# A Mamba block with an FP4 feed-forward on eight cores: other queues for the stores, and two buffers in the output projection

## The reference

```python
xn = _layernorm(x, axis=-1)
x = x + attn(xn) + ffn(xn)

# attn ("Mamba"): D_MODEL 1024, D_INNER 2048, D_STATE 16, DT_RANK 64, D_CONV 4
x = _rmsnorm(resid, norm_w)
skip = x @ skip_w.T
x = silu(_causal_depthwise_conv(x @ in_w.T, conv_w, conv_b))
delta = softplus(x @ wd1.T @ wd2.T + wd2_b)
Bm, Cm = x @ wb.T, x @ wc.T
y = _selective_scan(x, delta, Bm, Cm, A)      # h = exp(dt*A)*h + dt*x*B ; y = h.C
y = (y + x * W_D) * silu(skip)
return resid + y @ out_w.T

# ffn: every operand is quantized to FP4 in blocks of 16 and back
h = silu(fp4_linear(x, w_gate)) * fp4_linear(x, w_up)
return fp4_linear(h, w_down)
```

## Time and profile before

| | |
|---|---|
| median of 3 runs | 10604.0 us (10601.94 to 10607.22) |
| the profiled execution | 10596.79 us, of it the span of the slowest core 10595.3 us |
| spans of the 8 cores | 10570.5 to 10595.3 us |
| busy share of the span | DVE 58%, PE 27%, ACT 21%, POOL 10% |
| chain that ended last | DVE 56%, PE 13%, DMA 11%, issue 9%, ACT 9% |

### The profile page before, as it was taken

One profiled execution on the slowest core, in us unless ns is written; L12 is line 12 of the kernel. 1 busy time (PEld: TensorE's weight loads), 2 busy tenths in 40 slices (PEclk: granted clock), 3 DMA queues, 4 the chain that ended last, 5 costly groups with the idle time before them and its releaser, 6 DMA issues.

```text
span 10595.3 us, 50685 instructions; the slowest of 8 cores (10570.5 to 10595.3 us)
## 1 busy us (share of the span) xinstructions
PE 2895.6 (27%) x8880; PEld 961.4 (9%) x8880; DVE 6135.6 (58%) x5976; ACT 2235.5 (21%) x2910; POOL 1017.9 (10%) x680
## 2 busy tenths in 40 slices
PE   1111125545430333311111113333322222222224
PEld 0000011111110000000000001111000000000001
DVE  5656653434431222279999982222189997999940
ACT  1222211111123111123333321111122222222200
POOL 0000000000000000034444430000000000000000
PEclk9999996766665555555555556666555555555557
DMA  1111210010011100010000001111111112112122
GB/s 49 45 46 44 61 57 12 12 47 34 30 33 42 42 33 34 32 57 24 16 24 16 16 28 71 42 43 42 70 52 46 38 48 81 54 54 71 54 66 73
DMA packets 194274, 460.18 MB, mean 43 GB/s; under 512 B 114416, under 2 KB 115056, under 8 KB 170736
## 3 DMA queue, kind: packets, MB, share of 16 engines
q1 hardware_dynamic: 155760, 312.99, 9.3%
q0 software_dynamic: 38208, 143.94, 3.7%
HBM read 296.71 MB, written 160.17 MB: 43 GB/s over the span
## 4 chain that ended last, share of the span: by engine, by line
DVE 56%; PE 13%; DMA 11%; issue 9%; ACT 9%; DVEq 1%; ACTq 1%; SPq 0%; POOLq 0%
DVE s3o_hb L54 11%; DVE pf_ub L54 8%; DVE pf_E L54 6%; DVE s3o_ub L54 5%; DVE s3o_hcb L54 3%; PE c3o_pssk L825 2%; PE c3p_psx L759 2%; DVE c3o_cb L54 2%; DVE c3p_cb L54 2%; DVE q_t L54 2%; DMA sdelta<-c3p_db 2%; DMA sdelta<-c3o_db 2%; DVE p2q_t L54 1%; PE c_pso L1266 1%; PE c3o_psx L759 1%
## 5 line engine op out<-in xcount | busy, mean ns | idle before, releaser
L54 DVE TENSOR_TENSOR_SCAN s3o_hb<-s3o_ab,h_sb,s3o_ub 128x2048 bf16<-128x2048 f32 x256 | 1147.8, 4484 | 83.3 <-ACT s3o_ab L103 57.9
L54 POOL TENSOR_TENSOR pf_ub<-pf_dxt,pf_Brep 128x1536 f32<-128x1536 f32 x256 | 792.0, 3094 | 1022.1 <-DVE pf_E L54 761.0
L54 DVE TENSOR_TENSOR pf_ub<-pf_dxt,pf_Brep 128x512 f32<-128x512 f32 x256 | 802.6, 3135 | 26.7
L103 ACT ACTIVATE s3o_ab<-s3o_dt,A_sb 128x2048 f32<-128x2048 f32 x256 | 513.2, 2005 | 1426.4 <-DVE s3o_hb L54 1397.1
L103 ACT ACTIVATE pf_E<-pf_c,pf_bias,nA_sb 128x2048 f32<-128x2048 f32 x256 | 536.8, 2097 | 980.4 <-DVE pf_E L54 962.5
L1015 PE MATMUL s3o_psht<-eye_sb 128*128 128x128 bf16 x768 | 203.3, 265 | 1868.5 <-DVE s3o_hb L54 1163.6
L1198 PE MATMUL pf_psht<-eye_sb 128*128 128x128 bf16 x768 | 201.5, 265 | 1602.6 <-DVE pf_ub L54 1054.6
L54 DVE TENSOR_TENSOR s3o_ub<-s3o_dxt,s3o_Brep 128x2048 f32<-128x2048 f32 x256 | 586.8, 2292 | 27.0 <-DVE s3o_hcb L54 0.5
L54 DVE SCALAR_TENSOR_TENSOR pf_E<-pf_E,pf_ub 128x2048 f32<-128x2048 f32 x256 | 586.9, 2293 | 26.8
L103 ACT ACT_TABLE_LOAD x180 | 230.9, 1283 | 1477.2 <-PE p_psu L584 311.7
L54 DVE TENSOR_TENSOR p_h<-p_h,p_psu 128x512 f32<-128x512 f32 (+1 forms) x96 | 61.8, 644 | 746.1 <-ACT p_h L103 746.1
(11 more groups left out here) (175 smaller groups left out, 6156.5 us busy)
## 6 DMA issues: line engine op xcount, KB each, us to landing
s3o_dt<-sdelta SPq DMA_DIRECT2D x32, 1024.0 KB, 6.5
s3o_xct<-sxc SPq DMA_DIRECT2D x32, 1024.0 KB, 5.4
sxc<-c3p_xc POOLq DMA_DIRECT2D x64, 256.0 KB, 2.6
sdelta<-c3p_db POOLq DMA_DIRECT2D x64, 256.0 KB, 2.6
pf_dt<-sdelta SPq DMA_DIRECT2D x16, 1024.0 KB, 4.8
pf_xct<-sxc SPq DMA_DIRECT2D x16, 1024.0 KB, 4.8
sxc<-c3o_xc POOLq DMA_DIRECT2D x64, 256.0 KB, 2.6
sskip<-c3o_skb POOLq DMA_DIRECT2D x64, 256.0 KB, 2.6
```

What stands on the lines that cost most here:

```text
L54: instr = attr(*a, **k)
L103: scalar.activation(out=out, in_=in_, func=func, **kw).then_inc(kb.sems["S"], 1)
```

## The change

1. **Stores of the quantized weights** (stage 1) are started by ACT, right behind its last copy into `wide`, and counted on `Stg`; before, SP started them and counted on `St`. SP's load of `xb` still waits for `St`, which no longer counts them.
2. **Stores of `sxc`, `sskip`, `sB`, `sC`, `sdelta`, `sypart`, `sym`** (stages 4, 6, 7) are started by SP and counted on `St`; before, by POOL on `Stg`. The waits follow, and the one ahead of the copy into `dlowb` is gone.
3. **Output projection**: `outwT` is loaded by POOL into two buffers in turn; `ymt`, `rtile`, `ob` and the PSUM tiles exist twice. The load of tile `tt` waits for PE and DVE of tile `tt-2`, and for no store.

```diff
@@ gen_p0b
-            @B.sync
-            def _(sync):
-                kb.wait(sync, "S", ev)
-                kb.dma(sync, dst.rearrange(...)[...], wide[:].rearrange(...)[...], sem="St")
-            st_done = kb.cnt["St"]
+            @B.scalar
+            def _(scalar):
+                kb.wait(scalar, "S", ev)
+                kb.dma(scalar, dst.rearrange(...)[...], wide[:].rearrange(...)[...], sem="Stg")
+            st_done = kb.cnt["Stg"]
@@ feed-forward, before the loads of wgh, wuh, wdh
                 kb.wait(sync, "St")
+                kb.wait(sync, "Stg")
@@ p3_chunks, behind the first loop
                 sba.wait("Tn", t_dl)
-                sba.wait("Stg")
                 sba.act(dlowb[:], ps_dl[:], AF.Copy)
@@ p3_chunks, delta loop (sxc, sskip, sB, sC, sypart and sym likewise)
                     sba.wait("V", v_zb2)
-                    sba.wait("Stg")
+                    sba.wait("St")
                     sba.act(db[:], zb[:], AF.Exp)
                     s_db = sba.act(db[:], db[:], AF.Ln, bias=1.0)
 
-                    @B.gpsimd
-                    def _(gpsimd):
-                        kb.wait(gpsimd, "S", s_db)
-                        kb.dma(gpsimd, sdelta[...], db[:], sem="Stg")
+                    @B.sync
+                    def _(sync):
+                        kb.wait(sync, "S", s_db)
+                        kb.dma(sync, sdelta[...], db[:], sem="St")
@@ output projection, loads of outwT
-            @B.sync
-            def _(sync):
-                kb.wait(sync, "V")
-                kb.wait(sync, "S")
-                kb.wait(sync, "St")
-                kb.wait(sync, "Tn")
-                kb.dma(sync, tmpc[:], outwT.rearrange(...)[:, et, :])
+            @B.gpsimd
+            def _(gpsimd):
+                kb.wait(gpsimd, "V", oc_done[j])
+                kb.dma(gpsimd, oww_tmp[j][:], outwT.rearrange(...)[:, et, :], sem="Lg")
@@ output projection, token tiles
             @B.sync
             def _(sync):
-                kb.wait(sync, "V")
-                kb.wait(sync, "St")
-                kb.wait(sync, "Stg")
-                kb.dma(sync, ymt[:], sym.rearrange(...)[...])
-                kb.dma(sync, rtile[:], racc[tt * 128:(tt + 1) * 128, :])
+                kb.wait(sync, "Tn", t_os[j])
+                kb.wait(sync, "V", v_os[j])
+                if tt < 2:
+                    kb.wait(sync, "St")
+                kb.dma(sync, ymt[j][:], sym.rearrange(...)[...])
+                kb.dma(sync, rtile[j][:], racc[tt * 128:(tt + 1) * 128, :])
```

More of the change, by code:

```diff
@@ L807, in p3_chunks @@
                     v_xcf = kb.cnt["V"]
-                    @B.gpsimd
-                    def _(gpsimd):
-                        kb.wait(gpsimd, "S", s_xc)
-                        kb.dma(gpsimd, sxc[et * 128:(et + 1) * 128, c0:c0 + CH], xcb[:], sem="Stg")
+                    @B.sync
+                    def _(sync):
+                        kb.wait(sync, "S", s_xc)
+                        kb.dma(sync, sxc[et * 128:(et + 1) * 128, c0:c0 + CH], xcb[:], sem="St")
                     @B.tensor
@@ L832, in p3_chunks, with _ @@
                         sba.wait("Tn", t_bc)
-                        sba.wait("Stg")
+                        sba.wait("St")
                         s_sk = sba.act(skb[:], ps_sk[:], AF.Silu)
[L836 to L839, removed]
+                        @B.sync
+                        def _(sync):
+                            kb.wait(sync, "S", s_sk)
+                            kb.dma(sync, sskip[et * 128:(et + 1) * 128, c0:c0 + CH], skb[:], sem="St")
                 t_dl = kb.cnt["Tn"]
@@ L849, in p3_chunks, with _ @@
                 s_dl = sba.act(bcb[:, CH:2 * CH], ps_C[:], AF.Copy)
[L851 to L855, removed]
+                @B.sync
+                def _(sync):
+                    kb.wait(sync, "S", s_dl)
+                    kb.dma(sync, sB[:, c0:c0 + CH], bcb[:, 0:CH], sem="St")
+                    kb.dma(sync, sC[:, c0:c0 + CH], bcb[:, CH:2 * CH], sem="St")
                 for et in range(ET):
@@ L1036, in p3_scan, with _ @@
                             sba.flush(B)
[L1038 to L1041, removed]
+                            @B.sync
+                            def _(sync):
+                                kb.wait(sync, "S", s_y)
+                                kb.dma(sync, sypart[et * 128:(et + 1) * 128, :], ytl[:], sem="St")
                         else:
@@ L1059, in p3_scan, with _ @@
                             v_ym = kb.cnt["V"]
[L1061 to L1064, removed]
+                            @B.sync
+                            def _(sync):
+                                kb.wait(sync, "V", v_ym)
+                                kb.dma(sync, sym[et * 128:(et + 1) * 128, :], ymb[:], sem="St")
                     sba.flush(B)
@@ L1226, in build_nc @@
         oww = sb("c4_oww", [128, ET, D], BF16)
[L1227 to L1231, removed]
-        for et in range(ET):
-            @B.sync
-            def _(sync):
-                kb.wait(sync, "V")
-                kb.wait(sync, "S")
-                kb.wait(sync, "St")
-                kb.wait(sync, "Tn")
-                kb.dma(sync, tmpc[:], outwT.rearrange("(a p) d -> p a d", p=128)[:, et, :])
-            ldv = kb.cnt["L"]
+        oww_tmp = [sb(f"c4_owt{j}", [128, D]) for j in range(2)]
+        oc_done = [kb.cnt["V"], kb.cnt["V"]]
+        for et in range(ET):
+            j = et % 2
+            @B.gpsimd
+            def _(gpsimd):
+                kb.wait(gpsimd, "V", oc_done[j])
+                kb.dma(gpsimd, oww_tmp[j][:], outwT.rearrange("(a p) d -> p a d", p=128)[:, et, :], sem="Lg")
+            ldv = kb.cnt["Lg"]
             @B.vector
@@ L1261, in _ @@
                 kb.wait(tensor, "L", ldy)
-                kb.wait(tensor, "V")
-                kb.wait(tensor, "S")
+                kb.wait(tensor, "V", v_os[j] if v_os[j] else v_oww)
                 for ds in range(2):
                     for et in range(ET):
-                        mi = tensor.matmul(ps_o[ds][:], ymt[:, et, :],
+                        mi = tensor.matmul(ps_o[j][ds][:], ymt[j][:, et, :],
                                            oww[:, et, ds * 512:(ds + 1) * 512],
```

59 lines of the change are left out of this document (34 added, 25 removed).

## The result

The changed kernel takes 10403.2 us (median of 8 runs) against 10603.9 in the same comparison: a ratio of 0.981, 95% interval 0.980 to 0.982. That is 201 us off, where the prediction said 215 (10389, range 10325 to 10462). The profiled execution has a span of 10402.8 us on its slowest core, core 1; before it was core 5.

| stage, core 5 | before, us | after, us | difference | forecast |
|---|---|---|---|---|
| weights and first norm | 1465.5 | 1415.5 | -50.0 | -37 |
| feed-forward | 1632.2 | 1631.1 | -1.1 | 0 |
| norm of the prefix | 316.5 | 315.0 | -1.5 | 0 |
| projection of the prefix | 1092.8 | 1030.3 | -62.5 | -74.5 |
| state of the prefix | 1818.3 | 1819.8 | +1.5 | 0 |

A forecast was written before the change was run, and what follows sets the result against it. No engine is full; in the projections ACT waits for `sdelta` stores to land. Terms 122 + 27 + 37 + 8 + 18 + 3 = 215 us off 10596.8 give 10381.8, with the median 7.2 above: 10389, range 10325 to 10462.

The forecast's parts named there:

- What bounds the delta loop: Both projections: the next Exp waits for the `sdelta` store to land; the store alone closes a 4.72 us pass.
- The start: Delta loop: SP starts the store 0.12 us after Ln, POOL 0.59, so a pass gains 0.47 us.
- The landing: Delta loop: `sdelta` lands from SP in 2.05 us, not 2.6; with the sooner start, 122 us over 120 passes.
- the sign to look for: Delta loop: a pass of about 3.7 us in place of 4.72, with SP starting 0.12 us behind Ln.
- Rival 1: Delta loop: landing on SP stays at 2.6 us, so the loop gives 56 us; 146 in all, 10458; chance 0.17.
- The ends of the first loops: Both projections: shorter waits for the last store, sooner `sB` and `sC`; 27 us, ends 16 and 32.
- Stage 1: Token tile's load no longer waits for the weight store's landing: 37 us, at most 49, at worst 0.
- The 0.6 us for two transfers side by side: Stage 1: a 256 KB store moving at the same time may hold the token tile's load 0.6 us.
- Rival 2: Stage 1 and output projection's token tiles: side-by-side transfers hold each other up fully; 160 us in all, 10444; chance 0.10.
- The output projection: 8 us gained ahead of the first matmul, and 18 us between token tiles, 1.2 a tile, 15 times.
- The covers: Scan and state of the prefix: 0, wrong beyond 5 us; ACT loses 0 by issuing 52 stores more.
- The waits at the ends of stages: Three ends of stages, where SP waits for the last store, give 1 us each: 3.

The follow-up runs named there:

- e6: The changed kernel with two buffers for `db`, so that Exp waits for the store before the last: 10220.1 us, ratio 0.965.
- e10: The changed kernel with ACT starting the `sdelta` stores itself, its instructions emitted pass by pass, not one block for 16 passes: 10551.2 us in one run.
- e5: The changed kernel with each `sdelta` store split into two of 128 KB, one after the other: 10578 us in one run.
- e7: The changed kernel with the output projection's loads of tile `tt+1` ahead of tile `tt`'s store in SP's queue: 10246.9 us, ratio 0.967.
- e4: The changed kernel with SP again starting the quantized-weight stores, on the counter that the token tile's load does not wait for: 10409.9 us.

## Why the prediction was right, point by point

- **What bounds the delta loop** was right, and e6 shows it directly: with the wait for the landing moved away by one store, a pass falls from 4.03 to 2.48 us, which Exp, Ln and `zb` close.
- **The start** was right: 0.13 us for SP and, in e10, for ACT, against the 0.12 taken from other transfers.
- **The landing** is the term that was mis-sized: 2.05 us forecast, 2.35 measured. The step that failed started from SP's store of 512 KB (`out`, 2.64 us) and took off 0.6 us for half of the bytes, at the price of loads (1.2 us for 512 KB). Half of the bytes brought 0.3. A price alone doesn't mend the step: in e5 128 KB more cost this store 0.5 us, where the loads' price is 0.3, and with 0.5 the step would have given 1.6 us. So `out` and `sdelta` don't lie on one line, and the starting point was wrong too. What sets the two apart (their rows are 4 KB and 2 KB long) was not tried. So a pass gained 0.69 us and not 1.02 and takes 4.03, where the sign to look for was 3.7; and ACT's two waits, on core 5 before and after, shrank by 47 + 47 = 94 us where 122 stood. Rival 1, only the start gets shorter, would have been 56: the truth lay between the two. The Trainium skill's difference between the starting engines, 0.4 us ("DMA: Bandwidth & Descriptors", Specifications), gave 48 us; the rows show 0.46 us at the start and 0.23 in the landing.
- **The ends of the first loops** gave 124.6 - 94 = 30 us against 27. ACT's waits on core 5 show nearly the same directly: for the last store of the first loop 13.5 and 13.4 us before, none and 9.7 (now for PE) after; for `sC` 22.8 and 19.6 before, 13.9 and 14.1 after; 32 us in all. A store of 16 KB lands from SP in 1.4 us, 0.3 sooner than from POOL, where 0.2 was estimated.
- **Stage 1** gave 46 us between the medians of the eight cores (38 to 50 by core) in place of 37, and that is near the upper end of 49. The 0.6 us for two transfers side by side were not there: `p1o_x` lands in 4.2 us, 4.1 before. Rival 2 falls here.
- **The output projection** came out as forecast, on core 5 9.4 and 17.9 us against 8 and 18. Here a transfer did hold up another: `ymt` 5.1 us in place of 4.2, `out` 3.4 in place of 2.6, and the net was 1.1 to 1.6 us a tile by core. What was said of the two buffers, that they bring no more because the load stands behind the store, e7 shows: moving the load ahead brings 155 us.
- **The covers held**: scan and state of the prefix moved by 1.5 us on core 5 and by 4.1 at most on any core, where more than 5 would have spoken against the forecast. ACT lost nothing behind its stores that can be seen. On core 1 the view of waits does put five of its waits ahead of a token tile, 22.6 us, down to the landing of `swgT` and `swuT`; but the code waits there for the load alone, which is under way at the same time, and these waits are no longer than those put down to the load. The waits at the ends of stages can't be told from the noise.
- **The total is closer than its terms, and that is luck.** On core 5 the delta loop brought 28 us less than forecast, stage 1 13 more and the ends of the first loops 3 more, so half of the miss was made good by misses the other way.

## What to carry to other kernels

Where a store closes a loop, it pays a little to start it from a quicker queue and a lot not to wait for it: the queue brought 0.7 us a pass, a second buffer 1.5 more. A second buffer works only if the instruction that fills it stands ahead of the one that waits in the same queue; look at the order of the queue before trusting the buffer. And price a transfer by one of its own direction, rows and queue: the price of a load, taken off a store with other rows, was 0.3 us out in a landing of 2.35.

## What the runs showed that I had not expected

- The landing of equal stores from one queue can stay 1.1 us longer for ten passes (2.4 and 3.5 us in e6).
- Two transfers that start together from two queues did not slow the load in stage 1 (4.1 to 4.2 us), while in the output projection they cost each other 0.8 to 0.9 us. It isn't the queue: from one queue, in e4, the load of stage 1 landed in 4.2 us too. Sizes and rows differ between the two places, and what decides is open.
- A start of a transfer from SP that takes 0.33 us took 2.43 us right behind the 704 KB store in short pieces (e4).
- With ACT's instructions in one block for each pass and its own starts of the stores there was a table load of 1.28 us ahead of every Exp (180 to 300 loads in e10).
